# Three late groups of a graph layer's gathers handed from GpSimd to register-addressed transfers of ScalarE and SP

## What is computed

```python
def _mlp(h, W, b, gamma, beta):
    h = relu(h @ W + b)
    mu, var = mean(h, axis=0), mean(square(h - mu), axis=0)
    return gamma * (h - mu) * rsqrt(var + EPS) + beta

h = relu(layernorm(x))
node_feat = _mlp(h, W_node, ...)
edge_feat = _mlp(edge_attr, W_edge, ...)
message = _mlp(concatenate([h[row], h[col], edge_feat], axis=1), W_msg, ...)
out = x + segment_sum(message, col, 6250) + node_feat
```

## Time and profile before

| what | us |
|---|---|
| median of 3 runs | 1020.24 (1019.5 to 1021.5) |
| the profiled execution | 1019.37, of which its span is 1017.6 |
| PE busy | 757.2 |
| GpSimd busy | 751.2 |
| DVE busy | 529.4 |
| ACT busy | 361.7 |

### The profile page before, as it was taken

The page is one execution under the profiler, slowest core; times in us unless marked ns, Lnnn a source line. Parts: engine busy times, 40 slices in busy tenths (PEclk is TensorE's granted clock), DMA queues, the critical chain, the costliest instruction groups (busy, mean ns, idle before and its releaser), DMA issues.

```text
span 1017.6 us, 20372 instructions
## 1 busy us (share of the span) xinstructions
PE 757.2 (74%) x4800; PEld 617.0 (61%) x4800; DVE 529.4 (52%) x1401; ACT 361.7 (36%) x620; POOL 751.2 (74%) x786
## 2 busy tenths in 40 slices
PE   2605876662899999999999876777677776777777
PEld 2504652220788888888888765656566565666563
DVE  8796879997455555555555423222333332332225
ACT  4714788882333333333333311111112211211110
POOL 6887777777777777777777777777777777777770
PEclk9857898985799999999999978888787878978889
DMA  9574433335333333333333332222222222222223
GB/s 296 154 275 118 119 78 87 85 89 141 73 73 74 72 76 71 74 72 75 72 74 71 74 65 60 61 56 59 56 62 58 59 60 55 62 56 61 57 47 99
DMA packets 94002, 87.15 MB, mean 86 GB/s; under 512 B 65445, under 2 KB 70069, under 8 KB 93832
## 3 DMA queue, kind: packets, MB, share of 16 engines
q0 software_dynamic: 25024, 38.49, 17.6%
q1 hardware_dynamic: 68352, 47.05, 17.4%
q10 hardware_dynamic: 584, 1.22, 0.4%
HBM read 68.80 MB, written 14.54 MB: 82 GB/s over the span
## 4 chain that ended last, share of the span: by engine, by line
POOL 25%; issue 20%; DMA 14%; SPq 14%; DVE 10%; PE 9%; ACT 5%; ACTq 1%; DVEq 1%; POOLq 0%
POOL ring L467 25%; DMA ring<-p_table,src_idx 11%; SPq L439 9%; DVE edge_st L942 4%; ACT r_sb L578 3%; SPq L432 2%; PE pc L671 2%; DMA xs<-x_stack 2%; PE pd L774 2%; DMA big_a<-zeros 1%; PE pa L696 1%; PE pc L763 1%; SPq L430 1%; DVE ln_buf L857 1%; SPq L416 1%
## 5 line engine op out<-in xcount | busy, mean ns | idle before, releaser
L467 POOL DMA_INDIRECT ring<-p_table,src_idx x734 | 693.7, 945 | 223.8 <-issue 199.7
L774 PE MATMUL pd<-hm 128*97 128x193 f32 x1564 | 328.6, 357 | 116.7 <-ACT hm L626 116.6
L774 PEld LDWEIGHTS pd<-hm 128*97 128x97 f32 x1564 | 261.1, 177 | 135.7 <-ACT hm L626 96.9
L626 ACT ACTIVATE hm<-pc 128x384 f32<-128x384 f32 x196 | 96.4, 492 | 485.7 <-DVE pc L1016 481.8
L1016 DVE TENSOR_TENSOR pc<-pc,ring 128x384 f32<-128x384 f32 x196 | 110.6, 564 | 273.0 <-POOLq L494 251.6
L763 PE MATMUL pc<-w3q,r_sb 128*128 128x96 f32 x1564 | 232.8, 296 | 1.1 <-DMA w3q<-q_table 1.1
L763 PEld LDWEIGHTS pc<-w3q,r_sb 128*128 128x128 f32 x1564 | 208.9, 208 | 1.4 <-ACT r_sb L616 1.3
L1005 DVE TENSOR_SCALAR hm<-pb 128x384 f32<-128x384 f32 x196 | 109.1, 557 | 106.9 <-PE pb L748 58.3
L616 ACT ACTIVATE r_sb<-pa 128x512 f32<-128x512 f32 x196 | 116.4, 594 | 60.6 <-PE pa L742 57.8
L942 DVE BATCH_NORM_STATS2 edge_st<-r_sb 96x512 f32 (+1 forms) x196 | 121.2, 673 | 18.8 <-ACT r_sb L578 17.4
L742 PE MATMUL pa<-xs,we_stack 128*128 128x512 bf16 x196 | 84.1, 429 | 23.7 <-DMA xs<-x_stack 23.3
(11 more groups left out here) (112 smaller groups left out, 364.8 us busy)
## 6 DMA issues: line engine op xcount, KB each, us to landing
w3q<-q_table SPq DMA_DIRECT2D x782, 11.2 KB
ring<-p_table,src_idx POOLq DMA_INDIRECT x734
xs<-x_stack SPq DMA_DIRECT2D x98, 72.0 KB
x_stack<-ring SPq DMA_DIRECT2D x6, 980.0 KB, 7.6
xs<-x_stack SPq DMA_DIRECT2D x98, 60.0 KB, 1.8
ring<-in_x_nodes SPq DMA_DIRECT2D x5, 480.0 KB, 8.7
big_a<-zeros SPq DMA_DIRECT2D x1, 2400.0 KB, 13.4
p_table<-ring SPq DMA_DIRECT2D x12, 192.0 KB, 2.5
```

The lines of the kernel that those rows point to most:

```text
L467: nc.gpsimd.indirect_dma_start(out=ring[:, tile * C:(tile + 1) * C], out_offset=None, in_=table, in_offset=bass.IndirectOffsetOnAxis(ap=id ...
L626: nc.scalar.activation(hm[:, j, 0:n, WIN:WIN + C], pc[:, j % 2, 0:n * C].rearrange("p (t c) -> p t c", c=C), ACT.Relu).then_inc(msg_relu, 1)
L774: last = nc.tensor.matmul(pd[0:M1, j % 2, 0:HW], hm[:, j, t, WIN:HW], hm[:, j, t, :], start=(t == 0), stop=(t == n - 1))
```

## The change

Groups 189, 190 and 191 (`FAR`) are taken out of GpSimd's list (`by_pool`). Their 12 x 128 = 1536 rows are brought one by one into `far`, which lies in a buffer of the layer norm that is free by then: 86 rows of each tile (`FAR_BY_ACT`) by ACT, 42 by SP. For each partition the 12 row numbers are read from `src_idx` by one register load (`far_indices`), and each row is one transfer of 384 bytes. So ACT has 1032 such transfers and 86 register loads, SP 504 and 42.

`far_part` spreads them over the groups before 189: up to group 110 (`BACKLOG`) ACT issues 4 and SP 1 in each group, from there (1032 - 440)/79 = 7.5 and (504 - 110)/79 = 5.0. ACT's loop is written out for that. DVE waits for a far group on `far_in`, and for the others on `gathered` less the far groups before it; PE's and DVE's loops peel one turn more.

```diff
+FAR = tuple(range(NG - BODY - 3, NG - BODY))
+FAR_T = len(FAR) * TPG
+FAR_BY_ACT = 86
+BACKLOG = 110
...
+        def far_part(g, rows, early):
+            def due(h):
+                late = (rows * FAR_T - early * BACKLOG) * (h - BACKLOG) // (FAR[0] - BACKLOG)
+                return early * h if h <= BACKLOG else early * BACKLOG + late
+            return range(due(g), due(g + 1)) if g < FAR[0] else ()
+        def far_indices(engine, p):
+            at_tile = FAR[0] * TPG
+            _, at_node = nc.values_load_multi_w_load_instructions(
+                src_idx[p:p + 1, at_tile:at_tile + FAR_T], [engine], min_val=0, max_val=N, ...)
+            return at_node
...  (SP, after the w3q transfers of group g; ACT the same with FAR_BY_ACT rows and early = 4)
+                def load_far(n):
+                    p, t = FAR_BY_ACT + n // FAR_T, n % FAR_T
+                    if t == 0:
+                        far_nodes = far_indices(mybir.EngineType.SP, p)
+                    sp.dma_start(far[p:p + 1, t * C:(t + 1) * C], p_table[bass.ds(far_nodes[t], 1), :]).then_inc(
+                        far_in[t // TPG], 16)
+                    for n in far_part(g, P - FAR_BY_ACT, 1):
+                        load_far(n)
...  (GpSimd)
-                for g in range(RAW, NG + AHEAD):
+                by_pool = [g for g in range(RAW, NG) if g not in FAR]
+                for n in range(len(by_pool) + AHEAD):
...  (ACT)
+                for g in range(NG):
+                    keep_edges(0, g + 2)
+                    keep_messages(0, g + 1)
+                    for n in far_part(g, FAR_BY_ACT, 4):
+                        load_far(n)
-                passes(act, fast)
...  (DVE)
+                    if isinstance(g, int) and g in FAR:
+                        dve.wait_ge(far_in[g - FAR[0]], 16 * P * TPG)
+                        rows = far[:, (g - FAR[0]) * (TPG * C):(g - FAR[0] + 1) * (TPG * C)]
+                    else:
+                        dve.wait_ge(gathered, g + 1 - far_before(g))
+                        rows = ring[:, bass.ds((g % RING) * (TPG * C), n)]
```

More of the change, by code:

```diff
@@ L130, in graph_layer @@
         ln_w = ln_buf[:, 1, :].rearrange("p (s b) -> p s b", s=6)
+        far = ln_buf[:, :, :].rearrange("p a f -> p (a f)")[:, 0:FAR_T * C]
         ident_b = sb("ident_b", [P, P], bf16)
@@ L209, in graph_layer @@
         gathered = sem("gathered")
+        far_in = [sem(f"far_in{k}") for k in range(len(FAR))]
         x_main = [sem(f"x_main{k}") for k in range(2)]
@@ L272, in passes @@
             body(0)
-            with eng.Fori(1, LOOPS - 1) as i:
+            with eng.Fori(1, LOOPS - 2) as i:
                 body(i)
+            body(LOOPS - 2)
             body(LOOPS - 1)
@@ L287, in p1_passes, with far_before @@
             tail(P1_LOOPS)
+        def far_before(g):
+            return sum(f <= g for f in FAR) if isinstance(g, int) else 0
+        def far_part(g, rows, early):
[6 more added lines that the diff above has]
+            _, at_node = nc.values_load_multi_w_load_instructions(
+                src_idx[p:p + 1, at_tile:at_tile + FAR_T], [engine], min_val=0, max_val=N,
+                skip_runtime_bounds_check_because="a node of an edge, below N by the kind of input")
+            return at_node
         def p1_quads(i, k):
@@ L424, in _ @@
             with sp.If(outside < 1):
+                def load_far(n):
+                    nonlocal far_nodes
+                    p, t = FAR_BY_ACT + n // FAR_T, n % FAR_T
[3 more added lines that the diff above has]
+                        far_in[t // TPG], 16)
+                far_nodes = None
+                sp.wait_ge(src_in, 16)
+                sp.wait_ge(p_stored, 16 * NQ)
                 for g in range(NG):
@@ L480, in _ @@
             with pool.If(outside < 1):
-                for g in range(RAW, NG + AHEAD):
-                    if g < NG:
+                by_pool = [g for g in range(RAW, NG) if g not in FAR]
+                for n in range(len(by_pool) + AHEAD):
+                    if n < len(by_pool):
+                        g = by_pool[n]
                         if g == node_slot:
@@ L489, in _ @@
                         wait(pool, pre_added, g + 1 - RING)
[L490 to L493, removed]
+                        gather(g, p_table, gather_done[n % 4])
+                    m = n - AHEAD
+                    if m >= 0:
+                        pool.wait_ge(gather_done[m % 4], 64 * (m // 4) + 16 * tiles(0, by_pool[m]))
                         pool.sem_inc(gathered, 1)
@@ L632, in _, with load_far @@
                 keep_messages(0, 0)
[L634 to L637, removed]
-                passes(act, fast)
+                def load_far(n):
+                    nonlocal far_nodes
+                    p, t = n // FAR_T, n % FAR_T
+                    if t == 0:
+                        far_nodes = far_indices(mybir.EngineType.Activation, p)
+                    act.dma_start(far[p:p + 1, t * C:(t + 1) * C], p_table[bass.ds(far_nodes[t], 1), :]).then_inc(
+                        far_in[t // TPG], 16)
+                far_nodes = None
+                act.wait_ge(src_in, 16)
+                for g in range(NG):
[3 more added lines that the diff above has]
+                        load_far(n)
             with act.Else():
@@ L1014, in add_gathered @@
                     dve.wait_ge(pre_summed, g + 1)
-                    dve.wait_ge(gathered, g + 1)
-                    V.tensor_tensor(pc[:, j % 2, 0:n], pc[:, j % 2, 0:n],
-                                    ring[:, bass.ds((g % RING) * (TPG * C), n)], ALU.add).then_inc(pre_added, 1)
+                    if isinstance(g, int) and g in FAR:
[4 more added lines that the diff above has]
+                        rows = ring[:, bass.ds((g % RING) * (TPG * C), n)]
+                    V.tensor_tensor(pc[:, j % 2, 0:n], pc[:, j % 2, 0:n], rows, ALU.add).then_inc(pre_added, 1)
                 def add_sums(i, j, base):
```

## The result

The changed kernel takes 1095.39 us (median of 4 runs, 1093.26 to 1100.36) against 1020.61 of the kernel before on the same chip: a ratio of 1.074, with a 95% interval of 1.070 to 1.078. Forecast were 1163 us, in a range of 1065 to 1270. So the change is 75 us where 143 had been forecast (1163 - 1020), little more than half of it. The profiled execution, the slowest of the four, took 1100.36 us, its span 1098.6.

What follows compares the result with a forecast made beforehand. GpSimd's gathers were taken to bound the kernel before, SP's queue the changed one: 253.8 + 865 = 1119 us for the last `w3q`, 1144 of span, 1160 with 16 of contention, 1163 us of time; range 1065 to 1270.

Steps and rivals of the forecast that it cites:

- What bounds before, and SP's spare time: Main loop: GpSimd sets 5.0 us a group from about group 111; SP spares 0.06 us a group before, 2.2 after.
- What it removes: GpSimd's queue: twelve gathers fewer, 15 us; the end moves by 13 us where nothing else is late.
- A single row on SP: SP's queue: 369 ns a transfer, 0.55 us with register instructions and gaps, 277 us for 504 rows.
- The register load: SP's queue: a load of 12 row numbers takes 0.98 us with its gap, 41 us for 42.
- SP's own work: SP's transfers and register loads without single rows: 2.80 us a group, 547 us for 195.5 groups, starting at 253.8.
- Both queues at once: Contention of SP's and ACT's transfers: 16 us taken, between bounds of nothing and 264 us.
- the 0.58 to 0.68 that had the 78%: Main forecast: SP the bound at this many us a row, register load included, with little to moderate contention.
- rival 2: SP's rows cheap but not enough: at 0.39 to 0.5 us a row SP still sets the end, 1024 to 1082; 4%.
- Who waits: Main loop: PE's products of each group wait for late `w3q` transfers, then DVE and ACT in a chain.
- ACT: ACT's queue: 568 us of rows, 145 of register loads, activations hidden; done about 1000 us, 90 before SP.
- Rival 3: ACT becomes the bound, its single rows at the 697 ns of `we_stack`: 1358 us of time; 6%.
- Rival 1: GpSimd stays the bound, single rows in time; SP needs at most 0.38 us a row; full gain gives 1007; 7%.

Runs made afterwards that it cites:

- e1: Changed kernel without SP's 504 single-row transfers and 42 register loads, ACT's 1032 kept: 1008.77 us against 1017.82 of the kernel before, ratio 0.991.
- e3: Changed kernel with the 1536 rows shared otherwise: ACT 1248, SP 288 and none up to group 110, all issued one group earlier: 1004.73 us, ratio 0.986 to before.
- e10: As e3, but SP has 396 rows instead of 288, and ACT's early rows are 4 a group: 1043.59 us against 1020.68 before, ratio 1.023.
- e7: Kernel before plus extra transfers of 1 to 128 rows ahead of the main loop, on ACT and SP each alone, to price them: 1021.91 us.
- e2: Changed kernel without ACT's 1032 single-row transfers and 86 register loads, SP's 504 kept: 1091.40 us, ratio 1.072 to the kernel before.
- e9: Kernel before plus extra small transfers ahead of the main loop, from the chip's own memory and from DRAM, each queue alone; no run time given.

## Why the prediction was right, and which term was too large

- **What bounds before, and SP's spare time.** Right. The whole forecast stood on SP having no more than 2.2 us to spare in a group of 5.0. e1 (no rows on SP, back to GpSimd's pace), the doses of e3, e10 and the changed kernel (288, 396 and 504 rows on SP), and the queue that never stands still after show it.
- **What it removes.** Right: GpSimd's last gather moved by 14.9 us, and with SP out of the way the time fell by 9 us (e1, where the adds waited for single rows) and 13 (e3); 13 had been worked out.
- **A single row on SP.** The mis-sized term. 369 ns, from `bases`, were taken; 228 were measured. `bases` was taken as the nearest because it alone had one row, but it was issued by ACT beside SP's own five, and its row has 3920 bytes instead of 384; which of these made the 369 no run separates. The floor of 322, from transfers of 30 rows, was no floor: e7 shows that fewer rows cost less. This is 504 x (369 - 228) = 71 us too many.
- **The register load.** 0.98 us taken, 1.07 start to start measured: 4 us too few.
- **SP's own work.** 2.80 us a group taken, 554.5/195.5 = 2.84 measured, 7.5 us too few. The start was 257.1 instead of 253.8 in this execution, 3.3 us. From the last `w3q` (1069.7) to the last add were 6.6 us, not 3: 3.6 us. Start to start a row was 0.424 us in the mean, not the 0.41 of the median: 7 us.
- **Both queues at once.** 16 us taken. What there was of it is inside the terms measured above, so the whole 16 go out of the sum. By e2 it was 3.5 us of SP's queue and 2.3 between the last `w3q` and the last add (6.6 us here, 4.3 without ACT's rows).
- Together 1160 - 71 - 16 + 4 + 7.5 + 3.3 + 3.6 + 7 = 1098.4 us of span, measured 1098.6.
- **The range.** 0.51 us a row lies in neither case that was weighed: it is under the 0.58 to 0.68 that had the 78%, and just over the 0.39 to 0.5 of rival 2. The mechanism was right, the size wasn't, and the time lies in the range because that had been drawn down to 1065, two thirds up rival 2.
- **Who waits.** Not quite as told: PE stops for `xs`, not for `w3q`, since `xs` is the first transfer behind a group's single rows.
- **ACT.** Right that it wasn't the bound: its row took 213 ns, and its register load 992 where 1.69 us had been taken. Wrong that it would be done 90 us before SP: its last row starts at 1064.2 us, 5 us before SP's last `w3q`, since its rows stand behind its activations, which waited 152.8 us for PE's `pa` from 600 to 1070 us. So the adds of two far groups waited 5.1 us for them. Rival 3 took the 697 ns for its rows; e9 shows that they belong to another source.
- **Rival 1** needed 0.38 us a row. With 0.41 + 1.06/12 = 0.50 (0.51 in the mean) it was missed by a third, not by two thirds. With these prices (995.4 - 6.6 - 253.8 - 554.5)/0.51 = 354 rows are the break-even, an estimate; e10 with 396 rows lies 23 us over before, which gives 396 - 23/0.51 = 351. The changed kernel put 504 there, e3 288. The 50 ns that the prediction sets beside this rival are stated by the Trainium skill, "DMA: Bandwidth & Descriptors", section "Anatomy of one DMA — SWDGE (gpsimd) path", for GpSimd's path, so the 327 ns of SP's queue don't contradict them.

## What to carry to other kernels

A queue that only issues transfers has a budget like an engine: add up start to start what it issues in a period, and compare that with the period before work is moved to it, since all that follows in it waits for the least urgent row ahead. The work that is moved should go to the queue with the most room, here ACT; how the same 1536 rows were split between the two queues, and when SP's came, decided between 7% slower and 1.4% faster. And the price of a small transfer is to be taken from one of the same rows, source and addressing, or bounded well below the nearest one: here it was 228 ns, where the shortest transfer of SP in the trace of before had been 308.

## What the runs showed of the hardware that was not expected

- A single row of 384 bytes from DRAM, with its address from a register, holds SP's queue 228 ns and ACT's 213, against 328 for 30 rows. With fixed addresses it is 229 for 1 row, 387 for 16, 588 for 96 and 366 for 128 rows.
- With the source on the chip five partitions of 194 bytes cost at least 655 ns on SP and 697 on ACT, and a single row of 384 bytes, which goes as 16 pieces, at least 545 on SP (e9).
- With ACT's 1032 rows beside it (242 us of transfers) SP's queue took 813.1 us for its main loop, without them 809.6. In the changed kernel the 415 `w3q` that overlap a transfer of ACT took 342 ns in the mean, the other 367 took 334. The Trainium skill, "Perfetto Trace Analysis", section "DMA Instruction — HWDGE (DVE, Sync)", has the two share one descriptor generator with a lock, for which a transfer may have to wait; these 8 ns are the most that such a wait can have cost one of them in the mean.
- A register load of twelve values costs 1.04 us on SP and 0.99 on ACT, although that of a single value on ACT had taken 1.23 in the earlier trace rows.
